# A mixture-of-experts layer: GpSimd joins the halves of each tile's sum, and other Vector work stands between the Vector products

## The reference

```python
x = x + 0.5 * ffn(layernorm(x), Wg, We, be)      # mixture of experts
x = x + attention(layernorm(x), Wq, Wk, Wv, Wo, Wf)
x = x + 0.5 * ffn(layernorm(x), Wg, We, be)      # the same weights again

def ffn(x, Wg, We, be):                          # 8 experts, the 2 best are used
    probs = softmax(x @ Wg)                      # (tokens, 8)
    top_vals, top_idx = top_k(probs, 2)
    gates = top_vals / top_vals.sum(-1)
    expert_out = einsum('th,ehd->etd', x, We) + be[:, None, :]
    return sum over the 2 best of gate * expert_out
```

## Time and profile before

| what | value |
|---|---|
| median of 3 runs | 453.99 us (453.31 to 454.04) |
| the profiled execution | 452.93 us, of it 450.8 us span |
| PE busy | 395.8 us, 88% of the span |
| DVE busy | 364.8 us, 81% |
| ACT busy | 274.7 us, 61% |
| POOL busy | 252.4 us, 56% |

### The profile page before, as it was taken

One profiled execution on the slowest core, in us unless ns is written; L12 is line 12 of the kernel. 1 busy time (PEld: TensorE's weight loads), 2 busy tenths in 40 slices (PEclk: granted clock), 3 DMA queues, 4 the chain that ended last, 5 costly groups with the idle time before them and its releaser, 6 DMA issues.

```text
span 450.8 us, 11691 instructions
## 1 busy us (share of the span) xinstructions
PE 395.8 (88%) x3280; PEld 283.1 (63%) x3296; DVE 364.8 (81%) x1284; ACT 274.7 (61%) x758; POOL 252.4 (56%) x431
## 2 busy tenths in 40 slices
PE   0788888765799999999999999999999989888884
PEld 0666666542566776767677667767776657666652
DVE  3889999986867977887787779778766559999986
ACT  4667676543256575666666566756665756677653
POOL 8976666553155536644654555466445526675654
PEclk9999999997989999999999999999999999999999
DMA  4221000026554544464345535454640000010001
GB/s 116 78 75 21 4 1 0 1 84 169 135 147 120 158 116 142 129 172 114 122 137 153 135 105 157 116 158 115 172 117 5 4 2 0 26 47 24 23 23 48
DMA packets 45025, 39.13 MB, mean 87 GB/s; under 512 B 5128, under 2 KB 41756, under 8 KB 44986
## 3 DMA queue, kind: packets, MB, share of 16 engines
q1 hardware_dynamic: 44986, 38.66, 30.9%
HBM read 22.61 MB, written 15.20 MB: 84 GB/s over the span
## 4 chain that ended last, share of the span: by engine, by line
PE 48%; POOL 24%; issue 15%; DVE 8%; ACT 2%; DMA 2%; POOLq 1%; DVEq 0%; SPq 0%; ACTq 0%
POOL m_pair L217 10%; PE bank L917 9%; PE bank L902 9%; PE bank L887 8%; PE bank L890 5%; POOL m_upper L221 5%; PE bank L882 5%; POOL m_rstd L229 3%; DVE a_neg_max L795 2%; PE bank L1009 2%; PE bank L1012 2%; PE bank L961 2%; PE bank L926 1%; DMA x_all<-in_L_attn_x 1%; PE bank L1013 1%
## 5 line engine op out<-in xcount | busy, mean ns | idle before, releaser
L795 DVE TENSOR_REDUCE a_neg_max<-bank 128x2 f32<-128x512 f32 (+1 forms) x192 | 123.4, 683 | 46.2 <-PE bank L890 42.8
L684 POOL TENSOR_SCALAR_AFFINE_SELECT a_weights<-a_weights 128x512 f32<-128x512 f32 (+1 forms) x96 | 81.0, 844 | 94.5 <-ACT a_weights L738 93.4
L738 ACT ACTIVATE a_weights<-bank 128x512 f32<-128x512 f32 x192 | 104.9, 589 | 25.6 <-PE bank L902 25.0
L251 ACT ACTIVATE m_scaled<-bank,m_gates 128x128 f32<-128x128 f32 x256 | 72.3, 365 | 25.2 <-PE bank L417 25.2
L217 POOL TENSOR_TENSOR m_pair<-m_scaled 128x256 f32<-128x256 f32 x64 | 47.5, 742 | 50.1 <-ACT m_scaled L251 50.0
L902 PE MATMUL bank<-a_q_rows,a_k_rows 106*128 106x512 f32 (+1 forms) x192 | 71.2, 448 | 1.6 <-ACT a_weights L738 1.5
L294 DVE SCALAR_TENSOR_TENSOR m_lower<-bank,m_gates,m_lower 128x128 f32<-128x128 f32 x192 | 66.1, 344 | 2.3 <-issue 0.2
L887 PE MATMUL bank<-a_k_rows,a_q_rows 104*128 104x256 f32 x256 | 59.0, 333 | 0.4 <-DVE a_neg_max L795 0.4
L890 PE MATMUL bank<-a_mask,a_ident 128*128 128x256 bf16 (+1 forms) x176 | 56.2, 320 | 0.0
L917 PE MATMUL bank<-a_weights,a_v 128*32 128x128 f32 x1536 | 51.9, 276 | 0.0
L887 PEld LDWEIGHTS bank<-a_k_rows,a_q_rows 104*128 104x128 f32 x256 | 40.4, 193 | 14.6 <-DVE a_neg_max L795 10.6
(11 more groups left out here) (128 smaller groups left out, 824.3 us busy)
## 6 DMA issues: line engine op xcount, KB each, us to landing
a_k_rows<-k_stage SPq DMA_DIRECT2D x16, 416.0 KB
a_q_rows<-q_stage SPq DMA_DIRECT2D x64, 96.0 KB
k_stage<-a_k_parts SPq DMA_DIRECT2D x16, 256.0 KB, 2.2
q_stage<-a_q_parts SPq DMA_DIRECT2D x16, 256.0 KB, 2.3
a_k_heads<-k_stage SPq DMA_DIRECT2D x64, 52.0 KB
a_q_dense<-q_stage SPq DMA_DIRECT2D x16, 192.0 KB
x_all<-in_L_attn_x SPq DMA_DIRECT2D x8, 256.0 KB, 2.8
k_stage<-a_k_parts SPq DMA_DIRECT2D x16, 128.0 KB, 2.1
```

Of the source, the lines that this page charges most:

```text
L251: last = nc.scalar.activation(scaled[:, q % 2, j], y_high[q % 2][:, j * D:(j + 1) * D], ACT.Copy, scale=gates[:, s % 2, q, 4 + j:5 + j])
L684: nc.gpsimd.affine_select(out=diagonal, in_=diagonal, compare_op=ALU.is_ge, fill=0.0, base=0, pattern=[[0, heads.stop - heads.start], [1, P]],
L738: nc.scalar.activation(weights[n // 2][:, half:half + 4, :].rearrange("p h n -> p (h n)"), wt_bank[n % 2][:, :], ACT.Exp).then_inc(wt_exp, 1)
L795: nc.vector.tensor_reduce(neg_max[:, t, heads], score_bank[p % 2][:, :].rearrange("p (h n) -> p h n", n=(t + 1) * P), AX.X, ALU.max, negat ...
```

## The change

POOL does `finish` instead of DVE. It stands behind POOL's additions of the next tile (in quarter 0 behind `rstd_of` too), and it waits for product q.3 of its tile. Since `lower[q % 2, 3]` is now read by another engine, DVE waits before product q.3 of tile t until POOL has finished tile t-2. On DVE the statistics, aggregates, expert numbers and the remainder of the gates move in between the products of a chain.

```diff
         def part(i, s, q):                        # on POOL
             ...
+            if B and not (s == 0 and q == 0):
+                finish(i * Q + q - 1, (q - 1) % 2)
+            if q == 3 and s == G - 1:
+                finish(G * Q - 1, 1)
...
+        def finish(t, q):                         # now in gpsimd()
+            wait_apart(pool, low_chain, t * 4 + 4, pool_waited)
+            pool.wait_ge(upper_done, t + 1)
+            tile = x_all[:, bass.ds(t, 1), :].rearrange("p a d -> p (a d)")
+            nc.gpsimd.tensor_tensor(tile, lower[:, q % 2, 3], upper[:, q % 2], ALU.add).then_inc(upper_used, 1)
...
+            if j == 3:                            # in expert(), on DVE
+                at_least(dve, upper_used, t - 1)
...
-        def finish(t, q):                         # was in vector()
-
-            dve.wait_ge(upper_done, t + 1)
-            dve.wait_ge(low_chain, t * 4 + 4)
-            nc.vector.tensor_tensor(tile(t), lower[:, q % 2, 3], upper[:, q % 2], ALU.add).then_inc(upper_used, 1)
...
+        def statistics(g, tiles_of):
+            for k in tiles_of:
+                last = nc.vector.bn_stats(stats[:, k], tile(g * Q + k))
+            if Q - 1 in tiles_of:
+                last.then_inc(stat_done, 1)
+
+        def numbers(tiles_of):
+            for k in tiles_of:
+                last = nc.vector.max_index(best_no[:, k], best[:, k], logits[:, k])
+            if Q - 1 in tiles_of:
+                last.then_inc(no_ready, 1)
```

More of the change, by code:

```diff
@@ L332, in part @@
                 made["split_bias"](dve)
+            if q == 0 and B:
+                dve.wait_ge(bias_ready, i + 1)
+                xg = x_all[:, bass.ds(i * Q, Q), :].rearrange("p q d -> p (q d)")
+                nc.vector.tensor_tensor(xg, xg, bias_bank[:, :], ALU.add).then_inc(bias_added, 1)
+            if B:
+                if q == 0:
+                    dve.wait_ge(bias_added, i + 1)
+                expert(i, s, q, 0)
             if q == 0 and N and not early:
@@ L337, in part @@
                     dve.wait_ge(before["x_done"], 2 * m)
[L338 to L353, removed]
+                statistics(i + 2, range(2))
             if q == 1 and A:
@@ L374, in part @@
                 expert(i, s, q, 1)
+            if q == 0 and N and not early:
+                statistics(i + 2, range(2, Q))
             if q == 1 and A:
@@ L377, in part @@
                 nc.vector.tensor_tensor(gap[:, :], best[:, :, 1], best[:, :, 0], ALU.subtract).then_inc(chain, 1)
-                for k in range(Q):
-                    last = nc.vector.max_index(best_no[:, k], best[:, k], logits[:, k])
-                last.then_inc(no_ready, 1)
+                numbers(range(2))
+            if q == 3 and A:
+                after_link(n, 8)
+                nc.vector.tensor_tensor(gates3[:, 1], flat, gates3[:, 0].bitcast(FP32), ALU.subtract).then_inc(gates_ready, 1)
             if q == 2 and A:
@@ L385, in part @@
                 expert(i, s, q, 2)
-            if q == 3 and A:
-                after_link(n, 8)
-                nc.vector.tensor_tensor(gates3[:, 1], flat, gates3[:, 0].bitcast(FP32), ALU.subtract).then_inc(gates_ready, 1)
+            if q == 0 and N and not early:
+                wait_apart(dve, stat_done, m, waited)
+                for k in range(Q):
+                    last = nc.vector.bn_aggr(moments[:, b, k], stats[:, k])
+                last.then_inc(mom_done, 1)
+            if q == 1 and A:
+                numbers(range(2, Q))
             if q == 3 and N:
@@ L391, in part @@
                 nc.vector.tensor_tensor(xt_lo[:, b], xt_bank[:, :], xt_hi[:, b].bitcast(FP32), ALU.subtract).then_inc(lo_ready, 1)
-            if B and not (s == 0 and q == 0):
-                finish(i * Q + q - 1, (q - 1) % 2)
             if q == 2 and A:
@@ L402, in part @@
                                         g12[:, :, :].unsqueeze(3).broadcast_to([P, 2, Q, E]), ALU.mult).then_inc(chain, 1)
-            if q == 3 and s == G - 1:
-                finish(G * Q - 1, 1)
         return part
```

## The result

The changed kernel takes 462.32 us (median of 4 runs, 460.63 to 464.62), the kernel before on the same chip 453.75 us (453.31 to 454.04). The ratio is 1.0187, 95% interval 1.0158 to 1.0216: slower by 1.9%. I had predicted 457.7. The profiled execution took 462.01 us (span 460.3) against 452.93 (450.8).

The account below looks back on a forecast made before the run. DVE's own work bounded steady steps; two new waits would make them 10.34 us against 9.75. Ten periods + 5.9, less 0.7, 1.2 and 0.3, gave + 3.7 on 452.93; with 1.06 to the median 457.7, range 453.5 to 461.5.

Parts of the forecast that it names:

- Product 1.3 waits for POOL: DVE's product in quarter 1 of a steady step waits for POOL's finish of the step before, starting 0.75 us late.
- A: The start of the aggregates on DVE in a steady step, from which the prediction counted its times.
- Product 2.3 waits too: DVE's product in quarter 2 waits for POOL's finish of tile 0, starting at A + 4.90, 0.45 us late.
- POOL's finish takes 0.46: On POOL, one finish was put at 0.46 us, like `upper`, which has its shape.
- DVE's busy share 85%: In a steady step, DVE's busy share was to fall from 98% to about 85%.
- The bias addition waits for PE: DVE's bias addition waits for PE's bias product until about A + 8.05, standing still for 0.55 us or more.
- The remainder of the gates meets POOL: Rival, chance 0.20: DVE's L388 is held up by POOL, 0.2 to 0.7 us a meeting, 460.7 us in all.
- Wait 2: The bias addition on DVE waits for PE's chain behind product 2.3, to A + 8.05; ACT and loads not late.
- ten steady steps: Steps 1 to 6, five periods in each layer, each 0.59 us longer: + 5.9 us.
- beside attention: Steps 6 and 7 of the first layer, where DVE is rid of four finishes: an estimated - 1.2 us.
- into step 1 of the second layer: The statistics (0.78) stand ahead of a bias addition that could start almost at once: - 0.7 us.
- last two steps to the end: Steps 6 and 7 of the second layer: six tiles save 0.2 each, two finishes queue on POOL: - 0.3 us.

Follow-up runs that it names:

- e3: The changed kernel with POOL doing finish of the tile before ahead of adding up the next tile's upper half: 458.99 us.
- e4: The changed kernel with four buffers for the lower sums instead of two: 458.17 us.
- e7: e4 with all four statistics ahead of the bias addition again, the aggregates left behind product 0.2: 452.45 us.
- f1: e4 with quarter 0 on DVE as in the kernel before (statistics, bias addition, aggregates, then products): 449.10 us.
- f3: The changed kernel with quarter 0 on DVE as in the kernel before, two lower buffers and the wait for POOL kept: 452.60 us.
- e5: e4 with ACT normalising only the first 64 of 128 numbers of a token from step 1 on: 456.71 us.
- f4: The kernel before, DVE's order kept, with finish on POOL and four lower buffers: 450.12 us.
- e1: The changed kernel with finish back on DVE ahead of product q.3, DVE's new order kept: 467.05 us.
- e6: The changed kernel with two or three extra matmuls ahead of the experts of quarters 2 and 3 in steps 1 to 5: 458.84 us.

## Why the prediction was right in direction and short in size

**Step by step.** Product 1.3 waits for POOL: right, at A + 3.13 (I had A + 3.01), idle 0.80 (0.75). Product 2.3 waits too: wrong, at 61.10 it is A + 4.79, with no wait shown before it. DVE reached it later than I had worked out, 1.66 behind product 1.3 instead of 1.44, and POOL was earlier: `pair` started 0.41 behind the finish instead of 0.46, `upper` 0.81 behind `pair` instead of 0.89. POOL's finish takes 0.46: right, 0.457 at the median of 64. DVE's busy share 85%: right (9.01 of 10.57). The bias addition waits for PE: right, at A + 8.26 (I had A + 8.05). The remainder of the gates meets POOL: it does (62.51, 0.47 instead of 0.18), but PE's bias product starts 0.07 after L409's end at 63.83 and 0.14 after ACT's copy of the turned gates at 63.76, so at most 0.07 of it comes through. That rival's 460.7 comes nearest to the measured time, but for another reason.

**The step of the mechanism that failed** is in Wait 2: "ACT and the loads are not late: ... no term changes with it". ACT was looked at only up to the turned x. Its queue has `scaled` of tile 2 behind the four normalising instructions, and PE's next experts wait for that. That `scaled` ends at A + 5.26, and PE starts at A + 5.40. In the changed kernel this chain ends together with the one through product 1.3, so the sentence did not spoil the sum; it spoiled the cause. That the sum had the right path all the same is luck: I had followed one of two chains of equal length. By my account, taking the wait for POOL away should have brought the kernel back to 452.5 to 455, and e3 and e4 stayed at 459 and 458.2.

**The terms of the sum that failed** are the ten steady steps, which were sized too small, and the clock, which had no term. The span grew by 9.5 us, and I had + 3.7.

| term | predicted | measured |
|---|---|---|
| ten steady steps, without the slow clock | + 5.9 | + 8.7 |
| clock at 1.2 GHz in one step | none | + 2.3 |
| first layer up to bias addition 1 | none | + 0.2 |
| beside attention (from bias addition 6 of the first layer) | - 1.2 | - 1.0 |
| into step 1 of the second layer | - 0.7 | - 0.5 |
| last two steps to the end | - 0.3 | - 0.2 |

The ten steps grew by 6.49 and 4.46 us; 2.3 is what the 12.88 us step has over its 10.6 us neighbours. This 2.3 is read from one execution. The ten steps came out at 0.87 each instead of 0.59: the hand-offs behind a real wait cost more than I took. From the aggregates' end to POOL, 0.20 (56.68 to 56.88), where I had 0.08; from the bias product's end to the bias addition 0.18 (64.39 to 64.57), where I had 0.04; and bias addition to aggregates 2.37 instead of 2.29, with 0.81 to product 0.0 where I had 0.73. My 0.04 and my 0.73 came from the earlier trace rows, instructions outside the loops. The rest, beside attention and at the ends, was about right, except that the stretch beside attention also holds attention itself, and where in it the microsecond was gained stays open. Last, the median of the changed kernel lies 0.31 above its profiled execution and not 1.06 as before's did.

**The cause, as shown.** The aggregates behind product 0.2 start a circle over POOL, ACT, PE and DVE that is closed within the same step; the missing statistics expose its end. Putting the statistics back (e7), both back (f1, f3) or shortening the ACT link (e5) shortens the step; undoing the wait for `finish` (e3, e4) doesn't. What made the clock fall in one of the ten steps stays open.

## What to carry to other kernels

Before moving filler work between an in-order engine's instructions, ask of each piece whom it feeds and what it covers. Statistics and aggregates looked like filler, but three engines work on from them in turn, and PE's next experts start 5.4 us behind the aggregates. When two chains end together, a wait named by the profile is a candidate and not yet a cost. Take it away by a further buffer first, and if the step stays, look in the code for every other wait at the place where the chains join. Moving work off the busiest engine paid here (f1, f4) only with buffers enough that the busiest engine doesn't wait for its helper.

## What the runs showed of the hardware

**The clock can fall although the engine is busy for four fifths of the time.** Stretches of the changed kernel (clock is the column before the last two), and PE and DVE in them:

```profile
68.00:70.00 2.00, 1.65 (x6) 0.79 (x4) 1.27 (x13) 0.66 (x3) 1.74 (x5) 0.68 0.00 0
70.00:72.00 2.00, 1.52 (x4) 1.23 (x5) 1.85 (x10) 2.00 (x8) 1.55 (x3) 0.50 0.00 0
72.00:74.00 2.00, 2.00 (x9) 1.60 (x7) 0.65 (x5) 0.21 (x1) 1.59 (x3) 0.50 0.00 0
74.00:76.00 2.00, 2.00 (x8) 1.62 (x7) 1.83 (x7) 1.63 (x5) 0.00 (x0) 0.61 0.00 0
76.00:80.00 4.00, 3.55 (x22) 2.82 (x20) 2.43 (x11) 2.45 (x9) 2.80 (x5) 1.00 0.00 0
```

```profile
70.48 0.80 PE L430 MATMUL bank<-we_hi,m_xt_hi 128*128 128x512 f32 x1 [0.83 <-DVE m_lower L306]
71.07 0.63 PE L431 MATMUL bank<-we_hi,m_xt_hi 128*128 128x512 f32 x1
```

```profile
73.56 0.35 DVE L306 SCALAR_TENSOR_TENSOR m_lower<-bank,m_gates,x_all 128x128 f32<-128x128 f32 x1 [1.35 <-PE bank L431]
```

The granted clock is 0.50, the level of 1.2 GHz, from some 69 to 75 us; a matmul that takes 0.40 at 2.4 GHz takes 0.63, and product 3.0 waits 1.35 us for PE. In the step before, PE had been busy for 8.37 of 10.57 us, in pieces with idle times of 0.56 and 1.20 between them. Before the change it was busy for 8.56 of 9.74. e1 has one such step too, in the second layer: 13.06 us at a granted clock of 0.74. Steps with a mean clock of 0.84 to 0.86 stand in e3, e4 and e5 as well, and they are longer than their neighbours by 0.1 us (e4, 10.70 from 53.81 on) up to over 1 (e5, 11.80 from 74.98 on). In the changed kernel's second layer PE was busy for 42.13 of 52.94 us, the same share, and the clock stayed at 1.00; so the busy share alone doesn't settle it. Added matmuls (e6) kept the clock up.

**A DVE instruction with one SBUF input can stand still behind POOL.** In e4, L377, a `tensor_scalar` of 128x4 numbers, took 0.72 us (409.55 to 410.27) beside POOL's `pair` (409.50 to 410.24), and in the changed kernel, where it came at 60.09 just behind the `pair` (59.28 to 60.00), 0.16. In six more of e4's steps it took 0.70 to 0.72, each time starting 0.05 to 0.10 behind the start of a `pair`. The reciprocal behind it (L397), which has one SBUF input too, was not held: 0.16 at 410.44, in the midst of POOL's `upper` (410.31 to 410.77). This line isn't the L377 of my prediction, which counts by the kernel before and is the gap of the logits, with two inputs. The Trainium skill's "SBUF — State Buffer", section "SBUF: two separate sides", names DVE instructions in a 2-port performance mode beside those with two SBUF inputs as taking the exclusive lock; by that rule the trace agrees, if L377 ran in such a mode, which the rows don't say.

**A hand-off costs more inside the loops.** Steps 2 to 5 of a layer run in a register loop on each engine, the others as straight code. A bias addition that waits for PE's bias product starts 0.04 us after its end in the straight code (386.35 to 386.39) and 0.17 to 0.19 in the loop (396.63 to 396.80, 64.39 to 64.57). The two steps from a bias addition outside to the first one inside are 10.45 and 10.41 us long in the changed kernel, those inside mostly 10.6 to 10.7. Before the change DVE had no such wait in a steady step, so this cost was not exposed.
